# q computed in two pieces and W2 loaded in two pieces, in the opening of a ternary feed-forward kernel

## The reference

```python
q = relu(cond @ W3 + b3)                     # one row of 256 per sequence
s = x.sum(axis=1, keepdims=True)             # over the sequence's 32 rows
y = (32 * x + s) * q[:, None, :]
c = relu(y @ W2 + b2)
w1q, w3q, w2q = ternary(w1), ternary(w3), ternary(w2)
# ternary(w): m = mean(|w|); clip(round(w / m), -1, 1) * m
g = silu(c @ w1q.T) * (c @ w3q.T)            # 682 hidden features
out = x + g @ w2q.T
```

## Time and profile before

| | |
|---|---|
| median of 3 runs | 165.79 us (165.62 to 165.82) |
| profiled execution, its own time | 165.22 us |
| its span, first to last instruction | 163.4 us |
| TensorE busy, share of the span | 159.5 us, 98% |
| VectorE, ScalarE, GpSimd busy | 118.7, 89.1, 55.1 us |
| share of the last chain that is TensorE's | 97% |

### The profile page before, as it was taken

How to read it: one execution, slowest core, us unless ns; L and a number is a source line. 1 busy time by engine, 2 the same in 40 slices (tenths; PEclk the granted TensorE clock), 3 DMA queues, 4 the chain that set the end, 5 groups by cost and what they waited for, 6 DMA issues and landing times.

```text
span 163.4 us, 2290 instructions
## 1 busy us (share of the span) xinstructions
PE 159.5 (98%) x760; PEld 131.0 (80%) x760; DVE 118.7 (73%) x190; ACT 89.1 (55%) x163; POOL 55.1 (34%) x53
## 2 busy tenths in 40 slices
PE   8999999999999999999999999999999999999992
PEld 4798777888887888788887888788887888788892
DVE  1698999988978892798458891788548870566863
ACT  4077889344845375445844475345844466255540
POOL 5014022502460276205750276204841266001500
DMA  5998656665666599200240007000150006000163
GB/s 138 330 337 161 95 83 98 97 98 85 97 98 98 89 201 169 34 4 0 49 79 0 4 0 128 2 0 0 35 96 4 2 0 117 12 0 0 21 112 128
DMA packets 67412, 12.67 MB, mean 78 GB/s; under 512 B 63216, under 2 KB 67144, under 8 KB 67400
## 3 DMA queue, kind: packets, MB, share of 16 engines
q1 hardware_dynamic: 67248, 12.46, 39.2%
q10 hardware_dynamic: 152, 0.07, 0.2%
HBM read 8.32 MB, written 4.19 MB: 77 GB/s over the span
## 4 chain that ended last, share of the span: by engine, by line
PE 97%; DVE 1%; issue 0%; DVEq 0%
PE bank L553 50%; PE bank L596 22%; PE bank L483 15%; PE bank L580 3%; PE bank L469 2%; PE bank L518 1%; PE bank L445 1%; PE bank L498 1%; PE bank L452 1%; PE bank L510 0%; DVE qT L769 0%; PE bank L492 0%; PE bank L443 0%; DVE x L682 0%; DVE xo L821 0%; PE bank L521 0%
## 5 line engine op out<-in xcount | busy, mean ns | idle before, releaser
L553 PE MATMUL bank<-c_hi,T 128*128 128x512 f32 (+1 forms) x176 | 69.2, 393 | 0.0
L553 PE MATMUL bank<-c_lo,T 128*128 128x512 f32 (+1 forms) x176 | 68.8, 391 | 0.0
L389 ACT ACTIVATE silu<-bank,checked 128x512 f32<-128x512 f32 (+1 forms) x48 | 33.1, 689 | 51.5 <-PE bank L553 51.4
L806 DVE SCALAR_TENSOR_TENSOR gf<-bank,out_scale,silu 128x512 f32<-128x512 f32 (+1 forms) x42 | 31.2, 744 | 34.4 <-PE bank L553 30.8
L553 PEld LDWEIGHTS bank<-c_hi,T 128*128 128x128 f32 (+1 forms) x176 | 32.8, 186 | 7.6 <-issue 0.2
L553 PEld LDWEIGHTS bank<-c_lo,T 128*128 128x128 f32 (+1 forms) x176 | 32.8, 186 | 7.3
L272 POOL TENSOR_TENSOR x<-y,qT 128x512 f32<-128x512 f32 x12 | 13.7, 1144 | 53.2 <-DVE y L711 53.2
L596 PE MATMUL bank<-g_hi,T 128*128 128x512 f32 x70 | 28.5, 407 | 0.0
L814 DVE TENSOR_TENSOR g_lo<-gf,g_hi 128x512 fp32r<-128x512 f32 x40 | 28.5, 711 | 0.0
L396 ACT CAST g_hi<-gf 128x512 fp32r<-128x512 f32 x40 | 24.5, 612 | 5.4 <-DVE gf L806 5.1
L596 PE MATMUL bank<-g_lo,T 128*128 128x512 f32 x70 | 27.3, 390 | 0.0
(11 more groups left out here) (81 smaller groups left out, 118.1 us busy)
## 6 DMA issues: line engine op xcount, KB each, us to landing
xb<-in_x_dram SPq DMA_DIRECT2D x64, 64.0 KB, 2.5
out_dram<-turned SPq DMA_DIRECT2D x28, 128.0 KB, 2.7
xo<-in_x_dram SPq DMA_DIRECT2D x3, 256.0 KB, 4.4
w_sb<-in_L_ffn_w_dram SPq DMA_DIRECT2D x2, 384.0 KB, 5.5
w_sb<-in_L_ffn_w_dram SPq DMA_DIRECT2D x1, 682.0 KB, 7.8
w_sb<-in_L_ffn_w_dram SPq DMA_DIRECT2D x2, 256.0 KB
xo<-in_x_dram SPq DMA_DIRECT2D x1, 512.0 KB, 4.7
xo<-in_x_dram SPq DMA_DIRECT2D x2, 128.0 KB, 2.4
```

The lines of the kernel that those rows point to most:

```text
L389: nc.scalar.activation(silu[r, m % 2, :], h1[j % 2][r], ACT.Silu, scale=checked[r, 0:1]).then_inc(silu_done, 1)
L553: last = pe.matmul(dst[j % 2][0:w, :], T13[:, k, col:col + w], part[:, g % NC, k, :], start=(i == 0), stop=(i == len(passes) - 1))
L806: nc.vector.scalar_tensor_tensor(out=gf[r, m % 3, :], in0=second, scalar=out_scale[r], in1=silu[r, m % 2, :], op0=ALU.mult, op1=ALU.mult). ...
```

## The change

W2 is loaded by two transfers, one for each half of its input features, each with its own semaphore; TensorE waits for a half right before the products that read it, in the W2 product of half-group 0. q is computed in two pieces. The first piece, the 16 sequences of the first group, stays where q was, between the tiles of the first mixing, and VectorE applies bias and relu to it. The second piece, the other 112 sequences, goes behind the first mixing, in place of the three filler products, and into another bank (4 instead of 5); ScalarE applies its bias and relu, ahead of its first relu of a W2 product. VectorE (at scale_mixed) and TensorE (ahead of the first reduction) wait for it.

```diff
+    QF = HALVES * HB
-        qT_ps = bank[:, 5, 0:DC * B].rearrange("p (c b) -> p c b", c=DC)
+        q_first_ps = bank[:, 5, 0:DC * QF].rearrange("p (c b) -> p c b", c=DC)
+        q_rest_ps = bank[:, 4, 0:DC * (B - QF)].rearrange("p (c b) -> p c b", c=DC)
...
-            sp.dma_start(W2_sb[:], W2.rearrange("(c p) n -> p c n", p=P)).then_inc(got_W2, 16)
+            for k in range(DC):
+                sp.dma_start(W2_sb[:, k], W2[k * P:(k + 1) * P, :]).then_inc(got_W2[k], 16)
...
             act.wait_ge(b_cols_copied, 1)
+            act.wait_ge(q_done, 2 * DC)
+            for c in range(DC):
+                nc.scalar.activation(qT[:, HALVES:NH, c, :], q_rest_ps[:, c].rearrange("p (h b) -> p h b", b=HB), ACT.Relu,
+                                     bias=b3_col[c]).then_inc(q_rest_ready, 1)
...
                     if n == 0 and t == 1:
                         transpose_b()
-                        project_q()
+                        project_q(q_first_ps, slice(0, QF))
...
-            def project_q():
+            def project_q(q_ps, sequences):
                 pe.wait_ge(got_W3, 16)
                 pe.wait_ge(condT_copied, 1)
                 for c in range(DC):
-                    pe.matmul(qT_ps[:, c, :], W3_sb[:, c * P:(c + 1) * P], condT[:], start=True, stop=True
+                    pe.matmul(q_ps[:, c], W3_sb[:, c * P:(c + 1) * P], condT[:, sequences], start=True, stop=True
                               ).then_inc(q_done, 1)
...
                 for k in range(DC):
+                    if n == 0:
+                        pe.wait_ge(got_W2[k], 16)
                     if k:
...
             mix_x(0)
-            keep_busy(3)
+            project_q(q_rest_ps, slice(QF, B))
             mix_x(1)
-            pe.wait_ge(got_W2, 16)
             project_by_parts(0)
...
             pe.wait_ge(const_ready, 4)
+
+            pe.wait_ge(q_rest_ready, DC)
             sum_partitions(0)
...
             def scale_mixed(n):
+
+                dve.wait_ge(q_rest_ready, DC)
...
             for c in range(DC):
-                nc.vector.tensor_scalar(qT[:, :, c, :], qT_ps[:, c, :].rearrange("p (h b) -> p h b", b=HB), b3_col[c], 0.0,
-                                        ALU.add, ALU.max).then_inc(q_ready, 1)
+                nc.vector.tensor_scalar(qT[:, 0:HALVES, c, :], q_first_ps[:, c].rearrange("p (h b) -> p h b", b=HB), b3_col[c],
+                                        0.0, ALU.add, ALU.max).then_inc(q_ready, 1)
```

More of the change, by code:

```diff
@@ L146, in z_of @@
             return bank[:, b, :].rearrange("p (c n) -> p c n", c=DC)
-        got_cond, got_W3, got_W2, got_b = sem("got_cond"), sem("got_W3"), sem("got_W2"), sem("got_b")
+        got_cond, got_W3, got_b = sem("got_cond"), sem("got_W3"), sem("got_b")
+        got_W2 = [sem(f"got_W2_{k}") for k in range(DC)]
         got_w1, got_w3 = [[sem(f"got_w{k}_{part}") for part in range(2)] for k in (1, 3)]
@@ L163, in adaln_ternary_ffn_kernel @@
         b_cols_done, b_cols_copied = sem("b_cols_done"), sem("b_cols_copied")
-        q_done, q_ready = sem("q_done"), sem("q_ready")
+        q_done, q_ready, q_rest_ready = sem("q_done"), sem("q_ready"), sem("q_rest_ready")
         abs_done, sums_done, limit_done = sem("abs_done"), sem("sums_done"), sem("limit_done")
```

## The result

The changed kernel is slower: 166.32 us median of 22 executions (165.44 to 167.46), beside 165.68 of the kernel before on the same chips (164.86 to 166.14). The ratio is 1.0035, 95% interval 1.002 to 1.005. Forecast was 165.65, range 165.35 to 166.15. The medians hide the form: the 22 times fall into a tight group of nine from 165.44 to 165.78 and thirteen spread from 166.17 to 167.46, while the kernel before stays under 166.15. The forecast was added to 165.79; beside the 165.68 measured here it would be 165.54.

What follows compares the result with a forecast made beforehand. TensorE, carrying 97% of a 163.4 us span, was taken to bound the kernel. Of 0.15 us gained at the first W2 product the weights' gate passes 0.14: 165.79 - 0.14 = 165.65 us, range 165.35 to 166.15.

Steps and rivals of the forecast that it cites:

- First q product: On TensorE, 16 columns in place of 128: weight loads set the pace, gain 0.03 us, bounds 0 and 0.23.
- Rival A: Small q product worth more, 0.22 us more on TensorE, and the weights' gate open: time 165.42; chance 0.17.
- VectorE's evacuation: q's two bias-and-relu steps on 16 columns: 0.38 us in place of 0.61, gain 0.23, bounds 0.15 and 0.35.
- Second product: Rest of q behind the second tile's mixing: four passes of 112 columns, 0.44 us, replace fillers pushing the row by 0.17.
- The hole before the W2 product: TensorE's 0.47 us idle closes; its own order ends last, first W2 product could start at 6.76, today 6.94.
- ScalarE's two steps: Bias and relu of q's other 112 sequences in ScalarE's idle time: at most 0.84 us, price 0.
- W2 in two loads: One more SP issue, 0.47 us; DMA backlog keeps later landings unchanged: price 0, bounds 0 and 0.47 per landing.
- rival C: No early DMA backlog, so the third weight lands 0.47 us later, at 12.35: time 166.12; chance 0.06.
- The gates behind: Waits after the W2 product: 0.10 to 0.15 us passes x1's second part; the third weight's landing lets 0.14 through at most.
- The signs named beforehand: TensorE's load before W2 before 6.6: prediction falls; fast pace only after 5.4: rival B; third weight landing past 12.1: rival C.
- rival B: TensorE's fast pace comes only after the second mixing, 12 passes at half pace, 1.3 us later: time 166.9; chance 0.09.

Runs made afterwards that it cites:

- e8: The changed kernel once more, no edit, for a second profile: 165.79 us beside 165.61, ratio 1.0022.
- e5: The changed kernel with the first q product streaming all 128 columns again, only its first 16 used: 165.78 us, ratio 1.0023.
- e1: The kernel before with W2 loaded in two halves and nothing else: 165.75 us beside 165.70, ratio 1.0002.
- e3: The kernel before with one more 1 KB transfer on the SP queue behind W2's: 165.73 us beside 165.70, ratio 1.0004.
- e9: The kernel before with q's product on 16 columns, in place, q right for half-group 0 alone: 166.60 us beside 165.62, ratio 1.0053.
- e2: The changed kernel with W2 loaded whole again, q still in two pieces: 166.11 us, ratio 1.0016.
- e4: The changed kernel with half-group 3's load issued between the two parts of the first FFN weight: 166.78 us, ratio 1.0059.
- e14: e10 without the load of half-group 3, whose mixing reads half-group 2's rows (wrong output): 165.55 us beside 165.59, ratio 0.9997.
- e10: The changed kernel with the first q product on 128 columns and W2 in one load: 165.55 us beside 165.62, ratio 0.9996.
- e6: The kernel before with only q's bias and relu split between VectorE (16 sequences) and ScalarE (112): 165.44 us beside 165.61, ratio 0.9996.

## Why the prediction was wrong, point by point

- **First q product**: right. At the slow pace 16 columns save nothing (0.81 us for four loads in e8, 0.81 with 128 columns in e5), and at the fast one neither (0.44). Rival A's first half falls. The rule of the Trainium skill, "TensorE: Matmul & The Clock Gate", section "LDWEIGHTS (loading the stationary operand)", a load in its columns over 1.2, so 107 ns for 128, does not hold for these float32 loads at the slow pace: they stand 0.21 us apart.
- **VectorE's evacuation**: right, 0.38 for two.
- **Second product**: right in the price, 0.44 at the fast pace, but I costed it at that pace alone. At the slow one it is 0.83 (e8), for fillers of 0.31 (e1, from 6.62 to the next line at 6.93).
- **The hole before the W2 product**: right that it closes and that TensorE's own order takes q's place. Forecast 6.76, measured 6.35 with an early pace, 8.25 with a late one.
- **ScalarE's two steps**: right, 0.60 us in idle time, nobody waited.
- **W2 in two loads**: price 0 at the median, right (e1, e3). Part two, forecast near 6.32, landed at 7.02 in the first profile, and TensorE loaded for it at 7.06: in an early execution it has no slack. The landings did move: the third weight's first part (its issue plus the longer of the two landings) is there at 12.0 to 12.4 in six profiles with a second issue and 11.8 to 12.2 in six without, means 12.25 and 11.94. So of rival C's 0.47 some 0.3 is there, but in the medians of e1 and e3 it didn't reach the end.
- **The gates behind**: incomplete. I named the third weight and left out half-group 3, which in the profile of before had landed at 10.24, 0.45 us ahead of its use at 10.69. In five other kernels with the same issue time it landed at 10.6 to 11.0: that slack was the luck of one execution, and in the early executions this is the transfer that holds TensorE up longest. So the 0.14 that was to pass the gates did not pass: the tight group's median is 165.65, beside 165.68. That it is the forecast's own number is luck.
- **The signs named beforehand**: the load before W2 came before 6.6 (6.29 in the first profile), the third weight landed past 12.1, which was C's sign, and in e8 the fast pace came after 5.4, which was B's.
- **The step that failed: the chances, in rival B.** The mechanism was named, with the product that does it and a price of 1.1 us over the median. The measured price is 1.3 (166.90 beside the median of 165.61, and the same between the two profiles of the changed kernel); against the profile of the kernel before it is 1.7 in the span, as the slow pace also reaches into the W2 product, which B's sum left out. What was wrong is that I took it as one fate for the kernel (0.09) and argued that "the loads go on as densely". e9 leaves the loads as they were, and the high group is there. And it is drawn anew in each execution: 33 in 82 lie above 166.6. So it moved the median by 0.64, about half its price, instead of by nothing or all; in e8, with three of twelve, by 0.18. The range had been cut to leave just this case out, and 166.32 lies beyond its 166.15. The spread of the pace itself could not be seen from one trace; that a doubling sat inside the very product that was to be thinned out could, and should have weighed more.

That the narrow product brings the high group is shown by e9; that an execution of that group is one with a late pace, by the two profiles of one program and by e2 and e4. Why the early executions gain nothing is shown for those profiled only (waits for transfers), and it remains open for the typical one after e14. No version beat the kernel before: e10 and e6 equal it, with medians of 165.55 and 165.44 where the changed kernel has 166.32 and 165.79.

## What to carry to other kernels

In the stretch where TensorE's pace has not yet doubled, work that looks cheap to trim may not be: here narrowing one product saved nothing on the spot, and four executions in ten came out 0.9 us late or more. Look in the trace for the place where the distance of equal passes halves, and measure any thinning of what stands ahead of it over many executions. A slack against a transfer, read from one profile, has to be held against how that landing scatters: here by 0.7 us. And when the times of a kernel spread into groups, take a profile of each group before explaining the median.

## What the hardware showed unexpectedly

The column of the granted clock reads 1.00, the 2.4 GHz level, through all of this, also where passes go at half the pace they have later. Stretches of e8 (us, PE busy, granted clock, DMA share, GB/s):

```profile
core 0: us, PE busy (x), PEclk, DMA share, GB/s
4.00:6.00 2.00, 2.00 (x10) 1.00 0.83 235
6.00:8.00 2.00, 2.00 (x11) 1.00 0.97 309
8.00:10.00 2.00, 2.00 (x9) 1.00 1.04 346
```

The column misleads; the prediction, which met the contradiction in the earlier trace rows, rightly went by the pace. The column counts time for which the trace holds no clock record as full clock. Under it the packed trace keeps a list of granted clocks, and in twelve of the fourteen profiles (before and e10 have none) it begins with a record of 1.00 that starts just where the pace doubles, not at the start of the span: at 4.14 us in the first profile of the changed kernel, 9.24 in e8, 9.05 in e2, 10.34 in e4, 6.05 in e5, 6.9 in e1. So the pace is the granted clock, up to there at half, the 1.2 GHz level, which is nowhere recorded in the opening but follows from the distance of equal passes (0.21 us, then 0.11, for 128 columns of float32).

What TensorE did before the doubling: warm-up products, mixing and q from 0.8 us on, in all kernels without a hole of more than 0.3 us in its matrix rows. The late profiles differ on TensorE from those of the 128-column kernels up to 5.5 us only in the width of the first q product. One more number: six profiles with the same issue times had half-group 3 land over a range of 0.7 us.
